# One mixture-of-experts kernel: the experts' token lists made in two halves of eight, the first two experts run inside the second search

## The reference, cut to what matters

```python
T = 16 * 375                                  # 6000 tokens
cap = 375                                     # tokens that each expert takes
probs = softmax(x @ gate_w)                   # (T, 16)
scores, tok_idx = top_k(probs.T, cap)         # each expert picks its 375 best tokens
toks = xf[tok_idx]                            # gather
h = gelu(einsum(toks, w1) + b1)               # 128 -> 512
y = (einsum(h, w2) + b2) * scores             # 512 -> 128
routed = zeros.at[tok_idx].add(y)             # scatter-add
out = routed + gelu(xf @ sw1 + sb1) @ sw2 + sb2     # shared expert, every token
```

## Time and profile before

| what | us |
|---|---|
| median of 3 runs (lowest, highest) | 1312.71 (1312.13, 1312.76) |
| the profiled execution | 1312.21 |
| its span | 1310.5 |
| start of the third block | 1002.7 |
| last search step decided | 1069.3 |
| indices of all experts ready | 1109.0 |
| first scatter starts, last scatter starts | 1127.1, 1302.6 |

### The profile page before, as it was taken

How to read it: one execution, slowest core, us unless ns; L and a number is a source line. 1 busy time by engine, 2 the same in 40 slices (tenths; PEclk the granted TensorE clock), 3 DMA queues, 4 the chain that set the end, 5 groups by cost and what they waited for, 6 DMA issues and landing times. The chain is left out here.

```text
span 1310.5 us, 23146 instructions
## 1 busy us (share of the span) xinstructions
PE 1181.3 (90%) x7812; PEld 992.7 (76%) x7812; DVE 893.2 (68%) x2614; ACT 733.1 (56%) x1847; POOL 405.4 (31%) x379
## 2 busy tenths in 40 slices
PE   6999999999988999999999999999996998766663
PEld 6999999999966777777777777777764767555553
DVE  5656566656659898898998888988864887222120
ACT  2444534444448888888888888888882342222220
POOL 5000001202003442333344324231111001788885
PEclk9999999999999999999999999999997999878876
DMA  5100000000000000000000000000002110445442
GB/s 141 33 13 23 15 16 21 13 24 13 1 25 13 11 16 27 26 26 27 26 20 15 21 27 26 25 14 12 11 21 56 30 33 20 83 91 91 90 90 22
DMA packets 91799, 42.92 MB, mean 33 GB/s; under 512 B 31066, under 2 KB 88007, under 8 KB 91687
## 3 DMA queue, kind: packets, MB, share of 16 engines
q1 hardware_dynamic: 67207, 33.49, 9.4%
q0 software_dynamic: 23808, 6.69, 4.0%
q10 hardware_dynamic: 672, 1.31, 0.3%
HBM read 28.22 MB, written 9.65 MB: 29 GB/s over the span
## 5 line engine op out<-in xcount | busy, mean ns | idle before, releaser
L492 PE MATMUL bank<-h1hl,W2hl 128*128 128x376 f32 x1536 | 277.1, 336 | 2.9 <-DVE h1hl L648 2.9
L492 PEld LDWEIGHTS bank<-h1hl,W2hl 128*128 128x128 f32 x1536 | 263.4, 189 | 7.4 <-issue 4.3
L228 POOL TENSOR_SCALAR cellmax<-grid,csb 125x375 f32<-125x375 f32 x96 | 121.1, 1272 | 392.9 <-DVE csb L221 336.8
L1095 ACT ACTIVATE P<-P,nmax 125x375 f32<-125x375 f32 (+2 forms) x384 | 189.0, 509 | 2.4 <-DVE nmax L1236 2.2
L592 ACT ACTIVATE h<-bank,b2c 128x375 f32<-128x375 f32 x128 | 73.5, 575 | 207.1 <-PE bank L492 207.1
L1236 DVE CUSTOM_DVE_ANT_0 P<-bank,nbias 125x375 f32<-125x375 f32 (+2 forms) x384 | 139.0, 411 | 12.0 <-PE bank L913 12.0
L1105 ACT COPY PT<-bank 128x500 f32<-128x500 f32 (+1 forms) x256 | 128.5, 556 | 8.6 <-PE bank L926 7.9
L913 PE MATMUL bank<-QK 64*125 64x375 f32 (+2 forms) x768 | 116.2, 406 | 13.0 <-DVE nmax L1236 13.0
L926 PE MATMUL bank<-ident,P 125*128 125x125 f32 x768 | 113.5, 275 | 0.2 <-ACT PT L1105 0.2
L1714 ACT ACTIVATE hE<-bank,EB 128x375 f32<-128x375 f32 x64 | 36.7, 573 | 135.0 <-PE bank L1663 132.3
L1121 ACT ACTIVATE tap<-bank,qkd 128x375 f32<-128x375 f32 x128 | 68.5, 570 | 65.3 <-PE bank L962 65.2
(11 more groups left out here) (218 smaller groups left out, 2264.1 us busy)
## 6 DMA issues: line engine op xcount, KB each, us to landing
X<-in_x_dram SPq DMA_DIRECT2D x31, 375.0 KB
EW<-in_L_ffn_w_dram SPq DMA_DIRECT2D x32, 256.0 KB
token_table<-row SPq DMA_DIRECT2D x16, 210.9 KB
tTall<-tT SPq DMA_DIRECT2D x16, 187.5 KB, 2.5
out_dram<-oS SPq DMA_DIRECT2D x15, 187.5 KB
tTall<-in_L_tok_W_dram ACTq DMA_DIRECT2D x1, 1024.0 KB, 8.9
EB<-in_L_ffn_b_dram SPq DMA_DIRECT2D x16, 62.5 KB
tok<-token_table,ids POOLq DMA_INDIRECT x48
```

The lines of the kernel that those rows point to most:

```text
L228: nc.gpsimd.tensor_scalar(cellmax[:, k % 2], grid0[:], csb[:, TT_ + k:TT_ + k + 1], None, ALU.max).then_inc(s_cm, 1)
L492: last = nc.tensor.matmul(bank[4 + m % 2][:, :NE], W2hl[:, a, k, m * 128:(m + 1) * 128], h1hl[:, p, b, k], start=(k == 0 and n == 0), stop ...
L1095: nc.scalar.activation(P[:, 2 * r + q, SEG[i]:SEG[i] + w], P[:, 2 * r + q, SEG[i]:SEG[i] + w], ACT.Exp, bias=nmax[:, 2 * r + q, i:i + 1], ...
```

## The change

The 16 experts are split into two halves of eight. `probsT` becomes 128 rows (8 experts times 16 sequences) by 375 columns for each half, and SP stores two pieces of it for each sequence. The third block then does: search of half 0 (15 steps), lists of half 0, search of half 1 (15 steps), lists of half 1, experts 2 to 15. POOL issues the 24 gathers of half 0 while half 1 is searched, and the 24 of half 1 two at a time behind the scatters of experts 2 to 13. Expert 0 and the first layer of expert 1 are put into the last three steps of the second search, the second layer of expert 1 into the selection behind it. Two units of the shared expert stand in every search step (and two before the first). `shared_y` of sequence 0 moves from the end of the second block to just behind the last attention output. The experts' hidden layer uses two PSUM banks in turn in place of four; the bias of the second layer becomes a matmul with one row (three for each expert), and the score is multiplied straight out of PSUM. The output of the shared expert is added in place and no longer copied by ACT. The loops over experts are written out.

```diff
-                        sp.dma_start(probsT[m // 2 * E:(m // 2 + 1) * E, m % 2 * N:(m % 2 + 1) * N], pTs[:]
-                                     ).then_inc(s_ps, 16)
+                        for half in range(2):
+                            sp.dma_start(probsT[m * GE:(m + 1) * GE, half], pTs[half * GE:(half + 1) * GE]
+                                         ).then_inc(s_ps, 16)
...
+                        if (b, h) == (B, 3):
+                            shared_y(0, 0)
+                            shared_y(0, 1)
...
-                        if (b, h) == (B, 7):
-                            shared_y(0, 0)
-                            shared_y(0, 1)
...
-            STEP_UNITS = [(k + 1) * 45 // STEPS for k in range(STEPS)]
+            FIRST_UNITS = 2
+            STEP_UNITS = ([FIRST_UNITS + 2 * (k + 1) for k in range(STEPS)],
+                          [41 + 2 * (k + 1) for k in range(STEPS)])
+            LIST_UNITS = (33, 40, 41)
+            B_FROM = 2
...
+                def gather(e, k):
+                    pool.wait_ge(s_idx, e // GE + 1)
+                    nc.gpsimd.indirect_dma_start(
+                        out=tok[:, e % RING, k], out_offset=None, in_=table,
+                        in_offset=bass.IndirectOffsetOnAxis(ap=idx[:, e // GE, k, e % GE:e % GE + 1], axis=0)
+                        ).then_inc(s_ga[e % RING], 16)
+
+                def scatter(e):
+
+                    wait(pool, s_sc, 16 * NT * e)
+                    for k in range(NT):
+                        pool.wait_ge(s_ys, NT * e + k + 1)
+                        nc.gpsimd.indirect_dma_start(
...
+                for n in range(NT * GE):
+                    gather(n // NT, n % NT)
+                pool.wait_ge(s_first, 16 * HB)
+                pool.wait_ge(s_out, 16 * NB)
+                for e in range(E):
+                    scatter(e)
+                    for n in range(2 * (e - B_FROM), 2 * (e - B_FROM + 1)):
+                        if 0 <= n < NT * GE:
+                            gather(GE + n // NT, n % NT)
...
+                def second_layer(e):
+                    u = e % 2
+                    pe.wait_ge(s_ehr, 4 * e + 4)
+                    for t in range(NT):
+                        y = Y_B[min(t, 1)][:PT_, t * C:(t + 1) * C]
+
+                        if t < 2:
+                            wait(pe, s_ys, NT * (e - 1) + 1 if t == 0 else NT * e)
+                        for k in range(DC):
+                            nc.tensor.matmul(y, hE[:, u, k, t * PT_:(t + 1) * PT_], EW2[:, u, k], start=(k == 0),
+                                             stop=False)
+                        last = nc.tensor.matmul(y, ones_r[0:1, 0:PT_], EB2[0:1, u], start=False, stop=True)
+                        if t != 1:
+                            last.then_inc(s_ey, 1)
+
+                def search(half, done):
+                    for k in range(STEPS):
+                        pe.wait_ge(s_n, COUNTS * half + 3 * k + 3)
+                        nc.tensor.matmul(SMALL_B[:, TOT:TOT + 3], same[:], cnt[:, 0:3], start=True,
+                                         stop=True).then_inc(s_tot, 1)
+                        shared_units(done, min(STEP_UNITS[half][k], UNITS))
+                        done = min(STEP_UNITS[half][k], UNITS)
+                        if half and k == STEPS - 3:
+                            transpose_tokens(0)
+                            first_layer(0)
+                        if half and k == STEPS - 2:
+                            transpose_tokens(1)
+                            pe.wait_ge(s_yr, NB)
+                            second_layer(0)
+                        if half and k == STEPS - 1:
+                            first_layer(1)
...
+                shared_units(0, FIRST_UNITS)
+                search(0, FIRST_UNITS)
+                done = STEP_UNITS[0][-1]
+                place_totals(0)
+                shared_units(done, LIST_UNITS[0])
+                transpose_chosen(0)
+                shared_units(LIST_UNITS[0], LIST_UNITS[1])
+                collect(0)
+                transpose_lists(0)
+                make_indices(0)
+                shared_units(LIST_UNITS[1], LIST_UNITS[2])
+                search(1, LIST_UNITS[2])
+                place_totals(1)
+                transpose_tokens(2)
+                second_layer(1)
+                transpose_chosen(1)
+                collect(1)
+                transpose_lists(1)
+                make_indices(1)
+                for e in range(2, E):
+                    expert(e)
...
+                def take_tokens(e):
+                    dve.wait_ge(s_tp, e + 1)
+                    nc.vector.tensor_copy(tokT[:, e % 2], TOK_B[:, :N]).then_inc(s_tc, 1)
+
+                def weigh(e):
+
+                    wait(dve, s_sc, 16 * NT * (e - 1))
+                    for k in range(NT):
+                        dve.wait_ge(s_ey, 2 * e + min(k, 1) + 1)
+                        nc.vector.tensor_scalar(yE[:, e % 2, k], Y_B[min(k, 1)][:PT_, k * C:(k + 1) * C],
+                                                tok[:, e % RING, k, C + e:C + e + 1], None, ALU.mult).then_inc(s_ys, 1)
...
+                hot_b(0, SLOT)
+                pass_tiles(1)
+                pick(1)
+                for e in range(2, E):
+                    if e + 1 < E:
+                        take_tokens(e + 1)
+                    weigh(e)
```

More of the change, by code:

```diff
@@ L1603, in _ @@
-                last.then_inc(s_m, 1)
-                shared_units(done + 4, done + 10)
-                hotA2 = hotA[:].rearrange("p c a e -> p (c a e)")
-                def collect(j, first, final):
-                    for pair in range(PAIRS):
-                        for g in range(NG):
-                            c0 = j * PAIRS * E + pair * E + g * GE
-                            last = nc.tensor.matmul(LIST_B[g][:, 0:SLOT * GE], hotA2[:, c0 * AW:(c0 + GE) * AW],
-                                                    hotB[:, :, c0:c0 + GE], start=first and pair == 0,
-                                                    stop=final and pair == PAIRS - 1)
-                    return last
@@ L1642, in _, with place_totals @@
[L1642 to L1649 removed]
+                def place_totals(half):
+                    pe.wait_ge(s_sel, SELECTED * half + 2)
+                    nc.tensor.matmul(SMALL_B[:, 2:3], same[:], cnt[:, 1:2], start=True, stop=True)
+                    nc.tensor.matmul(SMALL_B[:, 3:4], before[:], cnt[:, 2:3], start=True, stop=True).then_inc(s_m, 1)
@@ new lines, in transpose_chosen @@
+                def transpose_chosen(half):
+                    pe.wait_ge(s_sel, SELECTED * half + 8)
+                    nc.tensor.matmul(SMALL_B[:, 4:5], before[:], place[:, N - 1:N], start=True,
+                                     stop=True).then_inc(s_m, 1)
+                    pe.wait_ge(s_sel, SELECTED * half + 9)
+                    for j in range(NT):
+                        last = nc.tensor.transpose(CHOSEN_B[:PT_, j * 128:(j + 1) * 128],
+                                                   chosen[:, j * PT_:(j + 1) * PT_], ident[:])
+                    last.then_inc(s_m, 1)
@@ new lines, in collect @@
+                def collect(half):
+                    hotA2 = hotA[:].rearrange("p c a e -> p (c a e)")
+                    pe.wait_ge(s_hot, LISTED * half + HOT)
+                    pe.wait_ge(s_c, 3)
+                    for c in range(NT * B):
+                        last = nc.tensor.matmul(LIST_B[:, 0:SLOT * GE], hotA2[:, c * GE * AW:(c + 1) * GE * AW],
+                                                hotB[:, :, c * GE:(c + 1) * GE], start=(c == 0),
+                                                stop=(c == NT * B - 1))
+                    last.then_inc(s_m, 1)
@@ L1684, in _ @@
             def _(act):
-                def gelu_shared(b):
+                for b in range(NB):
                     u = b % 2
@@ L1717, in _, with count @@
-                turns(act, turn)
+                for e in range(E):
+                    u = e % 2
+                    for m in range(DC):
+                        act.wait_ge(s_eh, 4 * e + m + 1)
+                        nc.scalar.activation(hE[:, u, m], H_B[m % 2][:, :N], ACT.Gelu_apprx_tanh,
+                                             bias=EB1[:, u, m:m + 1]).then_inc(s_ehr, 1)
             @block.vector
             def _(dve):
-                def count():
+                def count(half, bits):
@@ new lines, in decide @@
+                        dve.wait_ge(s_thr, base + 4 * n + 3)
+                        count(half, cand)
+                        if n > 0:
+                            ready = summed(STEP_UNITS[half][n - 1])
+                            add_shared(added, ready)
+                            added = max(added, ready)
+                        if half and n == STEPS - 3:
+                            take_tokens(0)
+                        if half and n == STEPS - 2:
+                            take_tokens(1)
+                            weigh(0)
```

(31 more changed lines are left out.)

478 lines of the change are left out of this document (173 added, 305 removed).

## The result

The changed kernel takes 1330.18 us (median of 4 runs, 1327.98 to 1337.55), against 1312.74 of the kernel before (1312.13 to 1317.06) beside it. The ratio is 1.0136, with an interval of 1.0089 to 1.0182: slower, and outside the range of 1303 to 1323. The profiled execution took 1328.25 us, with a span of 1326.5.

A forecast was written before the change was run, and what follows sets the result against it. POOL was taken to set the expert phase's pace, behind a serial lead. Tail 34.4 us less and lead 34.7 more gave a span of 1310.8; with 1.7 outside and 0.5 for the median, 1313.0 us, range 1303 to 1323.

The forecast's parts named there:

- the tail's last sentence: Expert phase, from expert 2's first scatter: PE needs 7.0 us an expert at full clock, under POOL's 10.5.
- The 7.0: PE's work per expert in us: first layer 2.99, second 2.79, bias 0.7, transposes 0.5.
- the sum: Whole kernel: longer lead and shorter tail give a span of 1310.8 us, time 1313.0, no measurable change.
- The pace of 10.5 us: Expert phase: time between experts' first scatters, set by the scatter's landing, in place of 11.53 us.
- The rival of 10.0: Expert phase: landing wait hidden behind the second gather, 10.0 us an expert, 6.5 less; faster case's chance 0.32.
- The lead: Everything up to expert 2's first scatter, put at 1161.8: 34.7 us more, for a second search.
- The counts over 375 columns: DVE's counts in each search step: 0.53 us apart, between bounds of 0.46 and 0.92.
- the rival of DVE beside POOL: Second search: each of 24 gathers costs a DVE instruction 0.42 us, 10 us in all, 1323; chance 0.13.
- PE at low clock: Searches, collecting and first layer: all low-clock stretches come whole, giving 1319 us; chance 0.15.
- the stretch that e8 filled: PE idle for 9 us ahead of collecting half 1: collecting taken as 6.4 us, against 4.29 at its shortest.
- PE sets the expert phase: Expert phase: PE at low clock takes about 12 us an expert, 19.5 more, 1332; chance 0.05.
- the other side, POOL slowing DVE: Second search and one-hot arrays: up to 0.42 us of a DVE instruction lost when POOL starts an indirect DMA.

The follow-up runs named there:

- e1: Changed kernel with five gathers of half 1 behind expert 1's scatters, then two behind each expert's: 1320.77 us, ratio 1.0042 to the kernel before.
- e2: Changed kernel with half 1's gathers begun behind expert 1's scatters, two behind each expert's: 1319.16 us, ratio 1.0032 to the kernel before.
- e9: Changed kernel with three gathers behind expert 2's scatters and two behind each later expert's: 1328.47 us, ratio 1.0106 to the kernel before.
- e3: Changed kernel with one gather fewer behind expert 2's scatters and three behind expert 13's: 1344.43 us, ratio 1.0222 to the kernel before.
- e4: Changed kernel, from expert 2 on each second layer ahead of the next expert's transposes, weighing ahead of token copies: 1318.06 us, ratio 1.0023 to before.
- e7: Changed kernel with three gathers behind each expert's scatters from expert 2 on until none is left: 1323.84 us, ratio 1.0072 to before.
- e8: e1 plus 14 matmuls with unread results on PE ahead of the collecting of half 1: 1317.30 us, ratio 1.0021 to the kernel before.
- e6: e1 with expert 2 also ahead of the last lists and the gather schedule moved one expert on: 1304.62 us, ratio 0.9932 to before.
- e10: e6 with each expert's second layer ahead of the next expert's transposes, expert 2 included: 1308.31 us, ratio 0.9951 to the kernel before.
- e5: e1 with `shared_y` of sequence 0 back at the end of the second block: 1321.29 us, ratio 1.0069 to the kernel before.

## Why the prediction was wrong, point by point

**The step that failed** is the tail's last sentence, "PE must keep up: an expert is 2.99 us for the first layer ... 7.0 us at full clock, under 10.5". It compares what PE works with POOL's pace, and takes the tokens as given. (The 7.0 is low too, which did no harm: PE takes 8.2 us for an expert at full clock, as from the first layer at 1168.75 to the next at 1176.94, since the three groups of the second layer take 1.14 and their biases 0.48 each.) The kernel before gathers three ahead with three behind each scatter; the new order has three needed and two issued, and the sum left the account of these out. It was there to be made from the change's own loop. The second layer of expert e stands behind the transposes of e + 1, for which 3(e - 6) of half 1's gathers must have landed; those issued up to expert e - 2 are 2(e - 3), and one that stands behind expert e - 1 lands 3.52 us after its issue, when expert e's first scatter is already due. At e = 12 it is 18 against 18, at 13 it is 21 against 20, and at 14 it is 24 against 22. The runs show it in four schedules (e1 or e2, e9, after, e3: 0, 2, 3 and 4 long intervals), 48.6 us for the last three experts where the sum had 31.5, and e4 shows the second half of the cause, the transposes ahead of the second layer.

**The pace of 10.5 us** was right: 106.1 us for ten intervals, where 105 were forecast, and 138.2 for 13 in e1 against 136.5. The rival of 10.0 falls, since at 1180.75 POOL stands 0.97 us idle until the landing. e7 shows what the choice of two behind each is worth.

**The lead** was right to 2.7 us in the profile of after, with the small errors of the table; in the profiles of e1 to e4, e7 and e9, whose instructions up to there differ at most in e1's five gathers, expert 2 starts 1.1 to 5.4 us behind the forecast (1162.85 to 1167.20). The counts over 375 columns stand 0.53 apart, as chosen between 0.46 and 0.92, and as wide while gathers run, so the rival of DVE beside POOL falls for them. **PE at low clock**: the stretch that e8 filled is worth 1.9 us, less than 0.2%, and was in the sum with 2.1. In the changed kernel the late gathers also make long ones (0.51 and 0.50 above). POOL's idle time adds up: 5.55 and 7.12 us ahead of the first scatters of 13 and 14, less 0.6 each, and 3.0 more than usual ahead of each second one, 17.4 in all beside the 17.1 of excess. The last two are the low clock's, by the groups of 2.07 us in place of 1.14. **PE sets the expert phase**, the rival at 1332 with 0.05, comes near in its time but not in its mechanism: PE idled, for tokens, and its clock fell behind that. An expert at the low clock (1224.47 to 1237.98, 13.5 us) held no scatter back while PE was ahead.

**What stays.** With the gathers mended (e1, e2, e4) the kernel is 0.2 to 0.4% slower than before, where the sum had it level; the profiled executions of e1 and before are 3.3 us apart in their spans (1313.8, 1310.5). Part of it is that the changed kernel's own profile shows the quickest lead of all. Some of that lies ahead of the third block: the last transposes of L991 start at 989.79 in it and at 990.32 to 994.38 in e1 to e4 and e6 to e10, at the same code. From its first to its thirteenth decision the second search took 34.5 us in the profiles of after, e5, e6 and e7, and 35.2 to 37.4 in those of e1 to e4 and e8 to e10, at the same code. In e1 some steps are longer by 0.7 to 0.9 us, and PE's small matmul is what DVE waits for, at a granted clock of 1.00:

```profile
1085.27 0.16 DVE L1717 TENSOR_SCALAR reached<-bank 128x3 f32<-128x3 f32 x1 [0.48 <-DVE thr L1738]
...
1088.83 0.16 DVE L1717 TENSOR_SCALAR reached<-bank 128x3 f32<-128x3 f32 x1 [0.73 <-PE bank L1636]
```

Why these steps are longer in some executions is open; no experiment was made on it.

## What to carry to other kernels

When a change spreads a supply over a loop, write down for each turn how many pieces have been issued and how many the next consumer needs, to the last turn: a rate below the need is first taken from the slack, where a trace shows it as an engine that waits for its input more and more without harm, and is paid at the end, with everything that waits behind it in order. Ask of each in-order engine what stands behind a wait that may come late; putting the work that the bottleneck needs ahead of the wait (e4) is as good as removing the wait (e1). And an engine's idle stretch in the lead is room for a whole unit of the tail: e6 put one expert there, and with the gathers mended that turned the change into a gain.

## What the runs showed of the hardware

One scatter is three times as long as the others. While DVE fills `hotB` in bf16, POOL's indirect DMA takes 5.90 us; most take 1.96 to 2.06:

```profile
1136.63 5.90 POOL L1504 DMA_INDIRECT out_dram<-yE,idx  x1 [0.30 <-issue]
1137.22 4.29 DVE L1796 TENSOR_SCALAR hotB<-fb 125x384 bf16<-125x384 bf16 x25
```

The same instruction takes 5.90 to 5.92 us in all eleven profiles with this order, so it is no accident of one execution. The scatter before it, beside `hotA`, takes 2.06. That DVE's work is the cause was not tried. The Trainium skill, DMA: Bandwidth & Descriptors, section SWDGE vs HWDGE vs iDMA, says that GpSimd writes the descriptors of its DMAs into SBUF state from which DVE locks it out in its two-port mode; the 5.90 beside 1.99 us would fit that rule, but no run here shows in which mode DVE worked. In the changed kernel nobody waits for this scatter; in e6 the next one does (4.20 us idle at 1148.70). POOL is full from there to expert 3's first scatter at 1161.71, whose rows DVE had ready at 1160.02, so of the 3.9 us at most 1.7 lie on the path. I had weighed the contention only for the other side, POOL slowing DVE, which the even counts don't show.
